# Layer 0's self-attention on one core: the places of the values' products and of the first-pass entries in TensorE's order

## The chip, the cores and the metric

The kernel runs on one core of a Trainium2 chip. The metric is the device time of one execution in microseconds (us), the median of several. TensorE is PE in the rows (PEld is its weight load), VectorE is DVE, ScalarE is ACT, GpSimd is POOL, and SP is the engine that issues most DMAs.

## What is computed

A two-layer decoder on x of 2 x 1024 x 256 with a context of 2 x 77 x 256. Each layer has self-attention, cross-attention and a mixture of experts, each behind a layer norm and added to x. Only layer 0's self-attention is touched; it has 16 heads of 16 elements, no mask, and a layer norm on each head's queries, keys and values:

```
q = _layernorm((x @ Wq + bq).reshape(b, s, NH, HD), q_scale, q_bias)
k = _layernorm((x @ Wk + bk).reshape(b, s, NH, HD), k_scale, k_bias)
v = _layernorm((x @ Wv + bv).reshape(b, s, NH, HD), v_scale, v_bias)
scores = jnp.einsum('bqhd,bkhd->bhqk', q, k) * HD ** (-0.5)
probs = jax.nn.softmax(scores, axis=-1)
out = jnp.einsum('bhqk,bkhd->bqhd', probs, v).reshape(b, s, NH * HD)
return out @ Wo + bo
```

## The kernel before

`attention(block, l, causal, ...)` (from line 793) builds the self-attention of both layers; layer 0 calls it with `causal=False`, layer 1 with `causal=True`. The work is cut into NU = 8 units, a unit being one sequence and G = 4 heads. Queries and keys are bf16 parts, stacked, so that one matmul over 96 rows gives the scores of a head at nearly fp32 accuracy.

A unit goes through two passes, and the first pass of one unit lies between the matmuls of the second pass of the unit before.

First pass: the maximum of each query's scores. It is made of entries in a list called `ring`, which PE and DVE take in the same order. A *fill* (`scores`, lines 927 to 939) is two matmuls of 512 columns (two heads, 128 queries, half the keys); DVE takes the maximum of each in one reduce (line 1119). A unit has 32 fills. After each 16 of them DVE makes the final maxima in three small steps (lines 1086 to 1098), PE turns them (*maxima*, `turn_maxima`, line 943), DVE copies them (line 1131) and SP stores them by four DMAs as two more rows of the query stack (line 891). The third kind of entry, *output* (`turn_output`, line 949), is four transposes of the finished sum of 512 queries, copied out of its bank by ACT (`copy_out`, line 1031); DVE normalizes it (lines 1106 and 1110). Entry n of the ring writes banks 2(n mod 2) and the next one, and may start when DVE is done with entry n-2 (line 958).

Second pass: 16 groups a unit (8 blocks of 128 keys for each half of 512 queries). In a group, for each of the 4 heads j, `second_pass` (line 974) makes one *score* matmul of 512 columns over 98 rows; the two additional rows subtract the maximum. ACT takes the exp of it (line 1040). Scores rotate over three banks, so a score waits for the exp three scores before it (line 972). When all four exps of a group are done, `weighted` (line 988) makes the *values' product* of that group: four heads side by side in the array, fp32, 8 instructions in the trace. It is issued one group late, behind the score with j = PV_AT.

PE's order is written out by hand (lines 1003 to 1017): ahead of each score it issues the ring up to `upto[u][gi * G + j]`. That list is built in lines 856 to 873. `goal` spreads the entries that are due by the end of a unit evenly over the unit's 64 places (in the first and last unit more of them early). Fills of the next unit begin in the unit before: in a unit 1 to 6, 32 fills, two maxima and two outputs are issued. By this rule a group has its fills either ahead of scores 0 and 2, or ahead of scores 1 and 3, and maxima take a place of their own, after which the two patterns change over. Outputs are put behind the entries of place j = 2 in groups 1 and 9. PV_AT is 1 in layer 0: the product comes behind the second score.

ACT takes the copy-out behind the exp of score j = OUT_AT = 2, in groups 0 and 8. PE waits for the rows of the first maxima at a unit's start, and for those of the second ahead of group 8.

SP's order in the stage: for each unit the rows of both maxima, then the loads of a later unit.

Of the kernel before, what the change touches and what calls it, by code (L numbers as in the profile page):

```python
# [32 lines left out]
G = 4  # L33
# [63 lines left out]
def build(nc, a, out):  # L97
    ctx = ExitStack()
    with ctx:
# [693 lines left out]
        def attention(block, l, causal, blocked=None, ahead=None):  # L793
# [23 lines left out]
            last_of = [max(i for i, g in enumerate(groups) if g[0] == half) for half in range(2)]  # L817
# [4 lines left out]
            def hilo(half):  # L822
                return mh[half].rearrange("p (j c t) -> p c j t", c=2, j=G)

            PV_AT = G - 1 if causal else 1
            OUT_AT = G - 1 if causal else 2
            FILL, MAX, OUT = range(3)
            feed = []
# [6 lines left out]
            due = []  # L835
# [5 lines left out]
            def goal(u, past):  # L841

                at0 = due[u - 1] if u else first_due
                if u in (0, NU - 1) and not causal:
                    soon = max(at0, feed.index((MAX, u, 1)) + 1)
                    if past <= early:
                        return at0 + round((soon - at0) * past / early)
                    return soon + round((due[u] - soon) * (past - early) / (1 - early))
                return at0 + round((due[u] - at0) * past)

            def width(gi):
                return BANK - groups[gi][2]
# [3 lines left out]
            ring = feed[:first_due]  # L856
            upto = [[] for _ in range(NU)]
            for u in range(NU):
                at0 = due[u - 1] if u else first_due
                at, past = at0, 0  # L860
                for gi in range(NGR):
                    for j in range(G):
                        past += width(gi) / G
                        upon = goal(u, past / WORK)
                        ring += feed[at:upon]
                        at = upon
                        if j == 2 and gi in (1, last_of[0] + 2):
                            half = 0 if gi > 1 else 1
                            if u or gi > 1:
                                ring.append((OUT, u if gi > 1 else u - 1, half))  # L870
                        upto[u].append(len(ring))
            ring += [(OUT, NU - 1, 1)]
            NR = len(ring)
            entry = {e: n for n, e in enumerate(ring)}
# [49 lines left out]
            def _(pe):  # L924
# [42 lines left out]
                def second_pass(u, gi, j):  # L967
                    r = u % NST
                    half, kt, lo = groups[gi]
                    n = (u * NGR + gi) * G + j  # L970
                    if n >= 3:
                        pe.wait_ge(*due_at("exp", n - 2))
                    bank = PS[:, 4 + n % 3, 0:BANK - lo]
                    pe.matmul(bank, kst[r][0:KM, j, kt * P:(kt + 1) * P], qst[r][0:KM, j, half * BANK + lo:(half + 1) * BANK],  # L974
                              start=True, stop=True).then_inc(sem(s + "_sc"), 1)

                def weighted(u, gi):
                    half, kt, lo = groups[gi]
                    if gi in diagonal:
                        pe.wait_ge(*due_at("past", u * len(diagonal) + diagonal.index(gi) + 1))  # L980
                    else:
                        pe.wait_ge(*due_at("exp", (u * NGR + gi + 1) * G))
                    if gi == 0:
                        pe.wait_ge(sem(f"{s}_v{u % NST}"), 16 * loads(l, u))
                    if kt == 0 and (u or half):
                        pe.wait_ge(*due_at("o", 2 * u + half))
                    for j in range(G):
                        mm = pe.matmul(PS[SLOT * j:SLOT * (j + 1), 7, lo:BANK], vst[u % NST][:, kt, j, :],  # L988
                                       prob[:, gi % 2 * G + j, lo:BANK], start=(kt == 0), stop=(gi == last_of[half]))
                    mm.then_inc(sem(s + "_pv"), 1)  # L990
# [12 lines left out]
                for u in range(NU):  # L1003
                    pe.wait_ge(*due_at("rows0", 16 * G * (u + 1)))
                    for gi in range(NGR):
# [3 lines left out]
                        for j in range(G):  # L1009
                            first_pass(upto[u][gi * G + j])  # L1010
                            second_pass(u, gi, j)
                            if j == PV_AT and gi:
                                weighted(u, gi - 1)
                            elif j == PV_AT and u:
                                weighted(u - 1, NGR - 1)
# [1899 lines left out]
        with nc.Block() as block:  # L2915
            prepare(block)
            ln(block, "ln03", "x_in", 16 * 4, banks=(6, 7))
            centre(block)
            turned, copied, blocked, valued = prepare_cross(block)
            qkv0(block, turned, copied, valued)  # L2920
            attention(block, 0, causal=False, blocked=blocked)
            ahead = cross_experts(block)
            attention(block, 1, causal=True, ahead=ahead)
# [29 lines left out]
```

## Time and profile before

| | us |
|---|---|
| median of 3 timed runs | 1839.29 (1837.18 to 1839.97) |
| the profiled execution | 1833.47 |
| its span, first to last instruction | 1831.6 |
| layer 0's self-attention, first score of unit 0 to last product | 147.50 to 549.45 |
| busy: PE, DVE, ACT, POOL | 1513.0, 1196.9, 977.4, 533.5 |

The profile is one execution. Times of rows are us from the start of the span. A row of the order of time gives the start, the duration, the engine and line, the operation and how many were merged (x2); behind it, in brackets, the idle time before it and what ended that. A merged row's duration runs from the start of its first to the end of its last instruction, and matmuls overlap: the end of one lies behind the start of the next. So for PE the distance from start to start is the measure.

### The profile page before, as it was taken

To read this page: it belongs to the slowest core of one execution; us is meant where nothing else is said; L and a number is where in the kernel's file an instruction comes from. 1 tells how busy PE (TensorE), PEld (TensorE's weight loads), DVE (VectorE), ACT (ScalarE), POOL (GpSimd) and SP (SyncE) were. 2 spreads that over 40 slices of the span, in tenths; PEclk is the share of its full clock that TensorE was granted. 3 is DMA by queue.
4 is the path that set the end of the run, shared out by engine and by line. 5 is a ranking of instruction groups with operands and counts; after the bars stand their busy time and mean duration, and the time that the engine had idled before them with its cause. 6 is when DMAs were issued, how large, how long until landed. Compare 5 with 4: busy or idle time off the path is not lost. (4 is left out here: it accounts for less than half of the span.)

```text
span 1831.6 us, 27871 instructions
## 1 busy us (share of the span) xinstructions
PE 1513.0 (83%) x8907; PEld 824.4 (45%) x8908; DVE 1196.9 (65%) x4538; ACT 977.4 (53%) x2014; POOL 533.5 (29%) x466
## 2 busy tenths in 40 slices
PE   5858999999985688888888779999987982389997
PEld 3512222222223466666665543333346761146665
DVE  6978877777715999999985167777615668311111
ACT  2835776677774566666666336666654551111121
POOL 1782000000001455556646452121211332331111
PEclk9968999999997899999999889999999995689999
DMA  7195223343000000000004535456120122621110
GB/s 218 58 232 73 32 34 100 43 93 47 1 27 1 1 1 1 1 1 2 1 2 96 106 127 71 65 102 89 43 92 1 18 41 41 221 95 40 49 42 6
DMA packets 116040, 106.02 MB, mean 58 GB/s; under 512 B 45811, under 2 KB 92987, under 8 KB 115902
## 3 DMA queue, kind: packets, MB, share of 16 engines
q1 hardware_dynamic: 110641, 93.83, 24.3%
q0 software_dynamic: 2640, 6.31, 0.9%
q10 hardware_dynamic: 2624, 4.19, 0.7%
q8 instruction: 69, 1.13, 0.3%
q14 instruction: 66, 0.54, 0.1%
HBM read 68.56 MB, written 36.41 MB: 57 GB/s over the span
## 5 line engine op out<-in xcount | busy, mean ns | idle before, releaser
L1119 DVE TENSOR_REDUCE arena<-banks 128x2 f32<-128x1024 f32 (+1 forms) x448 | 484.2, 1108 | 169.7 <-PE banks L935 114.9
L1040 ACT ACTIVATE arena<-banks 128x512 f32<-128x512 f32 (+3 forms) x896 | 444.5, 556 | 199.1 <-PE banks L974 192.8
L935 PE MATMUL banks<-arena 96*128 96x512 bf16 (+3 forms) x896 | 269.8, 377 | 42.4 <-DVE arena L1119 21.8
L974 PE MATMUL banks<-arena 98*128 98x512 bf16 (+3 forms) x896 | 273.1, 363 | 7.8 <-ACT arena L1040 7.8
L988 PE MATMUL banks<-arena 128*32 128x512 f32 (+3 forms) x1792 | 219.7, 562 | 13.1 <-ACT arena L1040 10.0
L2049 DVE MATCH_REPLACE8 arena<-arena 128x77 f32<-128x77 f32 x1024 | 213.9, 224 | 0.0
L935 PEld LDWEIGHTS banks<-arena 96*128 96x128 bf16 x896 | 77.5, 100 | 217.2 <-DVE arena L1119 128.6
L974 PEld LDWEIGHTS banks<-arena 98*128 98x128 bf16 x896 | 82.8, 98 | 180.1 <-ACT arena L1040 115.8
L2907 DVE COPY arena<-banks 128x1024 f32<-128x1024 f32 x23 | 28.2, 1225 | 197.2 <-PE banks L2841 197.2
L2041 DVE MAX8 arena<-arena 128x8 f32<-128x77 f32 x1024 | 149.6, 224 | 0.7
L1911 POOL TENSOR_SCALAR arena<-arena 128x256 f32<-128x256 f32 x32 | 17.8, 556 | 421.7 <-DVE arena L2029 421.7
L1908 POOL TENSOR_TENSOR arena<-arena 128x1232 f32<-128x1232 f32 x32 | 72.4, 2264 | 167.4 <-DVE arena L2049 165.8
L1636 PE MATMUL banks<-arena 128*128 128x256 f32 x512 | 116.7, 386 | 0.0
L1636 PEld LDWEIGHTS banks<-arena 128*128 128x128 f32 x512 | 97.1, 192 | 19.3 <-issue 5.9
L1071 POOL TENSOR_SCALAR_AFFINE_SELECT arena<-arena 128x512 f32<-128x512 f32 x64 | 40.7, 636 | 210.9 <-ACT arena L1040 210.7
L2856 PE MATMUL banks<-arena 128*128 x368 | 85.6, 385 | 1.4 <-DVE arena L2907 1.4
L2829 PE MATMUL banks<-arena 128*128 x184 | 84.5, 603 | 0.5 <-ACT arena L2881 0.5
L2049 DVE MATCH_VALUE_LOAD arena<-arena 128x8 f32 x1024 | 83.7, 82 | 1.7
L2856 PEld LDWEIGHTS banks<-arena 128*128 128x128 f32 x368 | 68.0, 190 | 19.3 <-issue 11.0
L2744 POOL DMA_INDIRECT decoded<-arena x23 | 22.6, 985 | 176.9 <-DVE arena L2899 175.4
L988 PEld LDWEIGHTS banks<-arena 128*32 128x32 f32 x1792 | 35.3, 108 | 84.1 <-ACT arena L1040 59.6
L2887 ACT ACTIVATE arena<-banks 128x1024 f32<-128x1024 f32 x23 | 23.6, 1024 | 86.1 <-PE banks L2832 86.1
(302 smaller groups left out, 2500.1 us busy)
## 6 DMA issues: line engine op xcount, KB each, us to landing
arena<-parts SPq DMA_DIRECT2D x192, 128.0 KB, 7.0
arena<-in_L_ffn_W SPq DMA_DIRECT2D x12, 1024.0 KB, 10.9
v<-arena SPq DMA_DIRECT2D x32, 256.0 KB, 3.4
arena<-v SPq DMA_DIRECT2D x16, 512.0 KB, 10.6
parts<-arena SPq DMA_DIRECT2D x12, 512.0 KB, 5.2
parts<-arena SPq DMA_DIRECT2D x16, 384.0 KB, 2.5
arena<-in_L_ffn_W ACTq DMA_DIRECT2D x4, 1024.0 KB, 9.5
arena<-sorted_rows SPq DMA_DIRECT2D x23, 129.0 KB, 2.2
```

What stands on the lines that cost most here:

```text
L935: mm = pe.matmul(bank[:, 0:w], qst[r][0:KS, j, i * P:(i + 1) * P], kst[r][0:KS, j, kb * BANK:kb * BANK + w], start=True, stop=not diag)
L974: pe.matmul(bank, kst[r][0:KM, j, kt * P:(kt + 1) * P], qst[r][0:KM, j, half * BANK + lo:(half + 1) * BANK], start=True, stop=True).then_i ...
L988: mm = pe.matmul(PS[SLOT * j:SLOT * (j + 1), 7, lo:BANK], vst[u % NST][:, kt, j, :], prob[:, gi % 2 * G + j, lo:BANK], start=(kt == 0), st ...
L1040: act.activation(prob[:, gi % 2 * G + j, lo:BANK], PS[:, 4 + n % 3, 0:BANK - lo], ACT.Exp, scale=SCALE).then_inc(sem(s + "_exp"), 1)
L1071: pool.affine_select(out=block_, in_=block_, compare_op=ALU.is_ge, fill=0.0, base=0, pattern=[[0, G], [1, P]], channel_multiplier=-1).then ...
L1119: dve.tensor_reduce(m2[u % 2][:, 2 * pair:2 * pair + 2, i, kb], PS[:, 2 * (n % 2):2 * (n % 2) + 2, 0:w], AX.X, ALU.max).then_inc(sem(s + " ...
L1636: mm = pe.matmul(PS[:, EB, 0:D], hmT[:, n, :], WeT[:, n // KD, n % KD, :], start=False, stop=(n == 2 * E - 1))
L1908: return pool.tensor_tensor(dst, src, m8[t % 2][:, 0, :, 0:1].to_broadcast([P, NH, C]), ALU.subtract)
L2041: dve.max(m8[r][:, k, hd, :], src[:, hd, :]).then_inc(sem(s + "_m" if k == 0 else f"{s}_m{k}"), 1)
L2049: dve.match_replace(out=left[r][:, hd, :], in_to_replace=m8[r][:, k, hd, :], in_values=src[:, hd, :], imm_value=LOWEST).then_inc(sem(f"{s} ...
L2829: pe.matmul(PS[:, 2 + half, :], xsT[r][:, k, :], W[:, bass.ds(e * EW + k * F + half * BANK, BANK)], start=(k == 0), stop=False)
L2856: pe.matmul(ps, lhs[:, k, :], weights[:, bass.ds(e * size + at + k * D, D)], start=(k == 0), stop=False)
```

## The change

Two things, in layer 0 alone (`not causal`); the order of layer 1 is built as before.

The values' product moves one score back: PV_AT is 2, so it stands behind the third score of a group.

The ring's entries no longer follow `goal`. A place `turned` takes entries up to and with the next fill; the others take none. Places with j = 3 are always turned; of the others j = 1, or j = 2 in a group with an output. In unit 0 groups 2, 5, 11 and 14 have j = 2 too (36 fills are due there). Outputs stand at j = 1 of groups 1 and 9, where there is no fill. Maxima come in the same place as the fill behind them: they are on top of the two fills of their group, where before they had a place of their own. A group is then: score 0; fill, score 1; score 2, product of the group before; fill, score 3. Group 4 and group 12 of units 1 to 6 have maxima and fill ahead of score 1. Groups 1 and 9: score 0; output, score 1; fill, score 2, product; fill, score 3. In unit 0 the first maxima entry in this stretch, the second of unit 0, moves from group 3 to group 5, into the place j = 2 of a group with three fills. In unit 7 all four fills are in groups 0 and 1, and the last maxima in group 2.

```diff
-            PV_AT = G - 1 if causal else 1
+            PV_AT = G - 1 if causal else 2
             OUT_AT = G - 1 if causal else 2
...
                 for gi in range(NGR):
                     for j in range(G):
                         past += width(gi) / G
+                        out = (OUT, u, 0) if gi == last_of[0] + 2 else (OUT, u - 1, 1) if gi == 1 and u else None
                         upon = goal(u, past / WORK)
+                        if not causal:
+
+
+                            upon = at
+                            turned = j == (2 if out else 1) or j == 3 or j == 2 and u == 0 and gi in (2, 5, 11, 14)
+                            while turned and upon < due[u]:
+                                upon += 1
+                                if feed[upon - 1][0] == FILL:
+                                    break
                         ring += feed[at:upon]
                         at = upon
-                        if j == 2 and gi in (1, last_of[0] + 2):
-                            half = 0 if gi > 1 else 1
-                            if u or gi > 1:
-                                ring.append((OUT, u if gi > 1 else u - 1, half))
+                        if out and j == (2 if causal else 1):
+                            ring.append(out)
                         upto[u].append(len(ring))
+                assert at == due[u]
```

## Rows read from the trace of the kernel before

**Rows 1.** Stretches (units 0, 3, 7, behind): PE, PEld, DVE, ACT, POOL busy, clock, DMA.
```profile
147.50:200.55 53.05, 50.34 (x263) 15.10 (x262) 43.58 (x47) 36.01 (x66) 1.20 (x1) 0.96 0.30 41
...
302.20:353.02 50.82, 47.77 (x268) 14.45 (x266) 40.01 (x45) 35.58 (x67) 0.00 (x0) 1.00 0.31 43
...
505.05:549.45 44.40, 37.69 (x211) 9.18 (x209) 8.13 (x13) 34.90 (x68) 0.00 (x0) 1.00 0.08 28
...
551.60:565.10 13.50, 9.06 (x26) 5.76 (x25) 0.85 (x3) 4.29 (x12) 1.16 (x2) 0.50 0.00 1
```

**Rows 2.** Order of time, PE, unit 3, output group: L974 score, L988 product, L935 fill.
```profile
305.03 0.60 PE L974 MATMUL banks<-arena 98*128 98x512 bf16 x2
306.21 1.06 PE L988 MATMUL banks<-arena 128*32 128x512 f32 x8 [0.58 <-ACT arena L1040]
307.21 0.61 PE L935 MATMUL banks<-arena 96*128 96x512 bf16 x2
...
308.09 0.60 PE L974 MATMUL banks<-arena 98*128 98x512 bf16 x2
309.14 0.60 PE L935 MATMUL banks<-arena 96*128 96x512 bf16 x2 [0.45 <-DVE arena L1119]
```

**Rows 3.** The same view, unit 3, around its maxima (L943).
```profile
315.07 0.23 PE L943 MATMUL banks<-arena 128*32 128x128 bf16 x1
315.23 0.39 PE L974 MATMUL banks<-arena 98*128 98x512 bf16 x1
316.03 0.61 PE L935 MATMUL banks<-arena 96*128 96x512 bf16 x2 [0.40 <-DVE arena L1119]
```

**Rows 4.** The same view, unit 3, groups without a stall.
```profile
319.31 0.38 PE L974 MATMUL banks<-arena 98*128 98x512 bf16 x1
319.62 1.07 PE L988 MATMUL banks<-arena 128*32 128x512 f32 x8
320.62 0.39 PE L974 MATMUL banks<-arena 98*128 98x512 bf16 x1
...
322.46 0.64 PE L988 MATMUL banks<-arena 128*32 128x512 f32 x4
```

**Rows 5.** Order of time, DVE, unit 3: reduces of fills.
```profile
307.85 1.23 DVE L1119 TENSOR_REDUCE arena<-banks 128x2 f32<-128x1024 f32 x1 [1.13 <-PE banks L935]
...
314.75 1.23 DVE L1119 TENSOR_REDUCE arena<-banks 128x2 f32<-128x1024 f32 x1 [0.48 <-PE banks L935]
```

**Rows 6.** Order of time, ACT, unit 3: copy-out (L1031) and exps (L1040).
```profile
305.08 0.58 ACT L1031 COPY arena<-banks 128x512 f32<-128x512 f32 x1
305.54 1.60 ACT L1040 ACTIVATE arena<-banks 128x512 f32<-128x512 f32 x3
308.51 1.09 ACT L1040 ACTIVATE arena<-banks 128x512 f32<-128x512 f32 x2 [1.37 <-PE banks L974]
```

**Rows 7.** Order of time, PE's weight loads: that of the second score of 305.03.
```profile
305.23 0.10 PEld L974 LDWEIGHTS banks<-arena 98*128 98x128 bf16 x1 [0.32 <-ACT arena L1040]
```

**Rows 8.** Order of time, PE and DVE, unit 7.
```profile
513.97 1.23 DVE L1119 TENSOR_REDUCE arena<-banks 128x2 f32<-128x1024 f32 x1 [1.12 <-PE banks L935]
...
515.98 0.22 PE L943 MATMUL banks<-arena 128*32 128x128 bf16 x1
...
517.69 1.06 PE L988 MATMUL banks<-arena 128*32 128x512 f32 x8
...
519.77 0.39 PE L974 MATMUL banks<-arena 98*128 98x512 bf16 x1 [0.26 <-ACT arena L1040]
520.26 1.06 PE L988 MATMUL banks<-arena 128*32 128x512 f32 x8
```

**Rows 9.** Order of time, SP and PE, start of the stage.
```profile
142.07 2.76 SPq L891 DMA_DIRECT2D arena<-arena  x4
...
146.72 1.01 PE L935 MATMUL banks<-arena 96*128 96x512 bf16 x2 [0.28 <-DMA arena<-arena]
...
152.94 0.64 PE L988 MATMUL banks<-arena 128*32 128x512 f32 x4
```

## The prediction

> **What bounds the kernel now.** I read the busy time of each engine by stretch first. The change touches layer 0's self-attention alone, so the question is which engine sets the length of one of its eight units. Unit 3 takes 50.82 us, with PE busy 47.77, DVE 40.01 and ACT 35.58 at the full clock of 2.4 GHz (granted 1.00) [rows 1]. PE is the bound, but 3.05 us are still idle in it, and its ends are modelled. So I went to the PE's own order of time and measured from start to start. A 512-column score or fill matmul is followed by the next one after 0.22 us (a fill, which is two of them, takes 0.44); a values' product that nothing holds up comes 0.31 after the score before it and lets the next matmul start 1.00 later; a group without a stall repeats after 2.84 us (319.62 to 322.46) [rows 2, 4]. Output transposes take 0.44: 307.21 to 308.09 is a fill (0.44) and four transposes [rows 2]. Maxima take 0.09 + 0.16 = 0.25 [rows 3]. A unit without stalls is then 16 x 2.84 + 2 x 0.44 + 2 x 0.25 = 46.8 us, so the unit of 50.82 holds 4.0 us of stalls. They stand at four places, two of each kind:
> - Output group (two a unit): scores at 305.03 and 305.25, so the product is due at 305.56 and comes at 306.21: 0.65. It waits for ACT, which put the copy-out (305.08) ahead of the group's last exp (305.54). Then the scores at 308.09 and 308.31 make the fill due at 308.53; it comes at 309.14: 0.60 to 0.61, waiting for DVE [rows 2, 6].
> - Maxima group (two a unit): maxima at 315.07, a score at 315.23, fill due at 315.45, comes at 316.03: 0.58 [rows 3]. What is left of the 4.0, some 0.17 each time, I put to the product of the pair order (two scores next to each other ahead of it, so that it needs a late exp).
>
> Both fill stalls are the same rule in the code: entry n of the ring may start when DVE is done with entry n-2. Reading a fill takes 1.23 us, starts 0.42 after the second matmul of the fill has started (307.85 against 307.43), and PE goes on 0.06 after its end: 314.75 + 1.23 + 0.06 is 316.03 [rows 2, 3, 5]. So a fill is ready 0.42 + 1.23 + 0.06 = 1.70 us after the second matmul of the fill two entries before it.
>
> **The change, part by part.** It adds and removes no instruction; it moves them on PE and, with the ring, on DVE. The new group on PE is: score 0, fill, score 1, score 2, product of the group before, fill, score 3.
>
> Plain group (12 of a unit's 16). From score 0: fill 0.22, score 1 0.65, score 2 0.87, product 0.87 + 0.31 = 1.18, fill 2.18, score 3 2.62, next score 0 2.84. That is the old stall-free length: nothing won. Three waits have to be hidden. Product: the last exp of the group before starts 0.42 after its score (308.51 against 308.09) and lets PE go 0.67 after it starts (305.54 to 306.21) [rows 2, 6]: score 3 stood at -0.22, so the product may go at 0.87, long before 1.18. Fills: ready 1.70 after the one before them at -0.44, that is 1.26, against 2.18; the other has more. Score 2 needs the bank that the group before's score 3 used (three banks): its exp ends at -0.22 + 0.42 + 0.60 = 0.80, and PE can go 0.05 later, 0.85; score 2 is due at 0.87. That margin is 0.02 and nothing covers it. The old order has the same spacing once in some groups: there the weight load of the score due at 305.25 waited for ACT until 305.23, and the matmul was not late [rows 2, 7]. I take zero.
> The Trainium skill (TensorE: Matmul & The Clock Gate, Step-by-step: what each phase is for) says that PE pulls weight loads ahead of matmuls in flight. If that were needed here, a load that waits until 0.85 and takes 0.10 would make every score 2 late by about 0.08; the row of 305.23 disagrees, the matmul going 0.02 behind the start of its load.
>
> Output group. The copy-out now waits on ACT for a product one place later. The product (start 1.18, 1.06 long) lets ACT go at about 2.28; ACT, with exps 0.5 apart, is free at 2.18, copies from 2.28 to 2.86 and can start the next instruction 0.46 after the copy's start (305.08 to 305.54), at 2.74, before the next exp is due at 2.62 + 0.42 = 3.04 [rows 2, 6]. Queued behind the waiting copy is only that exp, so the 0.65 goes. The transposes are due at 3.06, with the copy ready at 2.92: no wait. The fill now comes behind fill, score 3, score 0, four transposes, score 1: from the second matmul of the earlier fill 0.22 + 0.22 + 0.22 + 0.44 + 0.22 = 1.31, ready at 1.70: stall 0.39, in place of 0.60. Together 0.39 for 1.26 [rows 2, 6].
>
> Maxima group. Maxima and a fill stand in one slot: from the earlier fill's second matmul score 3 0.22, score 0 0.44, maxima 0.75, fill 0.91, ready 1.70: stall 0.79. Old 0.58 + 0.17. A loss of 0.04 each [rows 3, 5].
>
> Per unit: 2 x 0.39 + 2 x 0.79 = 2.35 of stalls for 4.0 (3.98 from the finer starts): 1.63 us less, so 49.2 us. Six units (1 to 6): 9.8 us. Bounds: the output's fill between 0 and the old 0.60, the maxima's between the old 0.58 and 0.79 plus one more 0.22: the six units give between 9.8 - 5.2 = 4.6 and 9.8 + 4.7 + 2.5 = 17; I take the worked-out values, since each is a sum of spacings seen next to each other in rows 2 to 5.
>
> Unit 0 runs its first 4.6 us at half clock (granted 0.96 over the unit), 0.43 a matmul [rows 1, 9]. The first entry stood at 146.72, held by the maxima's row DMAs; now score 0 stands there, and 13 matmuls (0.43 each, one of them 0.38) later the first product comes at 152.3 instead of 152.94, with two fills fewer behind it: 0.64 - 0.87 = -0.2. From 152.94 to the unit's end at 200.55 are 47.6 us; the work in it (15 products, 58 scores, 32 fills, an output, two maxima, at the spacings above) is 43.9, the stalls 3.7. The new order has 0.39 in the output group, 0.39 in each of three groups with three fills (one stands a group's end, 1.31, behind the fill two entries before it), about 1.3 where maxima and a fill stand two places behind another fill, and 0.1 at the other maxima: 3.0. Net gain 0.5. The second maxima of unit 0 move two groups later; their rows must land in the 7 us before group 8, and four such DMAs took 2.76 to issue and had landed 4.6 after the first issue [rows 9]. Unit 2's loads, queued behind them on SP, start some 6 us later; they are wanted by unit 2's first fill, in group 2 of unit 1, over 30 us on: no cost.
>
> Unit 7 has fills in its first groups only. Old: the product of group 3 comes 12.64 into the unit (517.69 against 505.05), the last product at 44.40, so 31.76 later [rows 1, 8]; the cycle is 2.57 (517.69 to 520.26). New: group 0 is 2.84 and the output group 2.84 + 0.44 + 0.39; the last fill's second matmul stands at 6.08, and the last maxima right behind it. From the start of that reduce to the maxima 2.01 pass in DVE's steps (513.97 to 515.98), so they come at 6.08 + 0.42 + 2.01 = 8.51, a stall of 1.68. Score 1, score 2, product, score 3 follow at 8.67, 8.89, 9.20, 10.20; its exp starts 0.42 later, lets score 2 go after 0.65 and the product 0.31 after that: 11.6. That last chain is the new cycle, 1.00 + 0.42 + 0.65 + 0.31 = 2.38, so the product of group 3 comes at 13.96, 1.3 late. From there eleven cycles, 2.08 to the last product (it needs no score 2) and about 0.3 for an output that waits for its copy make 28.6 in place of 31.76. Net gain 1.8.
>
> Sum: 9.8 (six units) + 0.5 + 1.8 = 12.1 us. The profiled execution had 1833.47 us around its span of 1831.6; 1821.4 by this. The three timed runs have a median of 1839.29, 0.3% more, and I carry the difference over: 1827.2 us. What follows, layer 0's cross-attention, starts from the last output transposes and should move as a block.
>
> **The rivals.** (1) The gain is partly given back behind the stage. PE falls to half clock (granted 0.50) for 13.5 us there with 9.06 busy [rows 1]; one more such stretch, because PE's idle times meet it otherwise, costs 4.5 us. For it: the clock changes at times that are not tied to the work; against: it may as well save one. 1830 to 1834.
> (2) Score 2 pays for its late bank: 0.08 in each of 112 groups, 9.0 us, gain 3: 1836.3. Against it stands rows 7.
> (3) Slower: the same score pays the load and then the 0.09 that a product pays on top of 0.22, 0.17 a group, 19 us: 1846. It decides from 12.1 / 112 = 0.11 us a group on.
> (4) The order doesn't do what it says: DVE, not the slot, sets the output and maxima stalls, so they only move: 1838 to 1840. Against: DVE needs 40.0 of 50.8 us.
>
> **How the numbers follow.** About 0.2% (3.7 us) is what can be told from no change. Forecast, 1824 to 1830: 0.75. (1) 0.10. (2) 0.06. (3) 0.05. (4) 0.04. Faster 0.85, same 0.10, slower 0.05. The range is 1824 to 1833.5: the forecast's case and most of (1).
>
> **What would show it.** Unit starts 49.2 us apart; a copy-out that begins right at the product's end, with no product waiting for ACT behind it; fills by 0.39 late in output groups and 0.79 in maxima groups; unit 7's cycle 2.38, maxima by 1.7 late there. A plain group over 2.84 is rivals (2) or (3), to be seen at score 2. The stage's last product should end 12 us earlier; if it does and the total doesn't, it is (1). The forecast is wrong if a wait that I hold hidden appears, above all score 2's.

## The result, and the profile after

The changed kernel takes 1824.35 us (median of 4, 1823.76 to 1825.56), the kernel before 1838.45 in the same comparison (median of 4, 1837.18 to 1839.97). The ratio is 0.9924 with a 95% interval of 0.9907 to 0.9941: 14.1 us or 0.76% faster. Forecast were 1827.2 us and 12.1 us less, with a range of 1824 to 1833.5; the measured time lies 0.35 us above the lower end of that range.

The two profiled executions tell another number, 1833.47 and 1824.05, only 9.4 us. So the profile has to be read in pieces. The first rows are times from the start of the span, the others are lengths; a unit is measured from its first score.

| us | before | after | difference | forecast |
|---|---|---|---|---|
| first product of unit 0 starts | 152.94 | 151.57 | -1.4 | -0.6 |
| unit 1 starts | 200.55 | 198.67 | -1.9 | -0.5 |
| last product of the stage starts | 549.45 | 536.59 | -12.9 | -12.1 |
| units 1 to 5, each | 50.82 | 49.17 | -1.65 | -1.63 |
| unit 6 | 50.39 | 49.17 | -1.2 | -1.63 |
| unit 7, first score to last product | 44.40 | 42.92 | -1.5 | -1.8 |
| last output transpose to layer 1's first score | 544.4 | 542.0 | -2.4 | 0 |
| from there to the first tile of the last stage | 511.7 | 512.0 | +0.3 | 0 |
| last stage (layer 1's experts) | 223.8 | 229.5 | +5.7 | 0 |

The stretches that answer to rows 1 (columns as there: length, busy time and instructions of PE, PEld, DVE, ACT, POOL, then the granted clock, DMA share and GB/s), of the kernel after; units 0, 3 and 7, and behind the stage:

```profile
146.70:198.67 51.97, 49.60 (x262) 14.92 (x263) 43.59 (x47) 35.10 (x65) 1.73 (x2) 0.96 0.31 41
297.00:346.17 49.17, 47.28 (x267) 14.31 (x266) 40.01 (x45) 34.68 (x66) 0.00 (x0) 1.00 0.32 44
493.67:536.59 42.92, 37.03 (x210) 8.94 (x208) 8.04 (x13) 35.07 (x67) 0.00 (x0) 1.00 0.08 29
536.60:546.60 10.00, 4.98 (x26) 2.82 (x27) 0.85 (x3) 4.07 (x10) 0.89 (x2) 1.00 0.00 1
546.80:550.00 3.20, 2.74 (x11) 2.05 (x10) 0.00 (x0) 0.80 (x3) 0.06 (x1) 0.50 0.00 0
```

PE in order of time, unit 3 of the kernel after: L983 score, L944 fill, L997 product, L958 output, L952 maxima. First a plain group and the output group, then the maxima group.

```profile
297.65 0.59 PE L983 MATMUL banks<-arena 98*128 98x512 bf16 x2
298.18 1.06 PE L997 MATMUL banks<-arena 128*32 128x512 f32 x8
299.18 0.61 PE L944 MATMUL banks<-arena 96*128 96x512 bf16 x2
299.62 0.60 PE L983 MATMUL banks<-arena 98*128 98x512 bf16 x2
300.05 0.61 PE L958 MATMUL banks<-arena 128*128 128x128 f32 x4
300.50 0.38 PE L983 MATMUL banks<-arena 98*128 98x512 bf16 x1
301.10 0.61 PE L944 MATMUL banks<-arena 96*128 96x512 bf16 x2 [0.22 <-DVE arena L1128]
301.55 0.38 PE L983 MATMUL banks<-arena 98*128 98x512 bf16 x1
301.86 1.06 PE L997 MATMUL banks<-arena 128*32 128x512 f32 x8
...
304.69 1.07 PE L997 MATMUL banks<-arena 128*32 128x512 f32 x8
...
307.53 1.06 PE L997 MATMUL banks<-arena 128*32 128x512 f32 x8
308.53 0.61 PE L944 MATMUL banks<-arena 96*128 96x512 bf16 x2
308.97 0.59 PE L983 MATMUL banks<-arena 98*128 98x512 bf16 x2
309.50 0.23 PE L952 MATMUL banks<-arena 128*32 128x128 bf16 x1
310.45 0.61 PE L944 MATMUL banks<-arena 96*128 96x512 bf16 x2 [0.73 <-DVE arena L1128]
```

Where rows 2 had a product 0.65 late and a fill 0.60 late, the products now come 0.31 behind the score before them, and one fill is late: due at 300.50 + 0.22 = 300.72, it comes at 301.10, 0.38. In the maxima group (rows 3: 0.58) the fill is due 0.16 behind the maxima, at 309.66, and comes at 310.45, 0.79 or 0.80 by the rounding. Both are 1.70 us after the second matmul of the fill two entries before: 299.18 + 0.23 + 1.70 = 301.11, and 308.53 + 0.23 + 1.70 = 310.46. Plain groups repeat after 2.84 (304.69 to 307.53), as in rows 4. Nothing else is late in the unit.

ACT in order of time, the same place (L1040 copy-out, L1049 exp), and the weight load of score 2:

```profile
297.20 2.07 ACT L1049 ACTIVATE arena<-banks 128x512 f32<-128x512 f32 x4 [0.77 <-PE banks L983]
299.31 0.58 ACT L1040 COPY arena<-banks 128x512 f32<-128x512 f32 x1
300.04 1.58 ACT L1049 ACTIVATE arena<-banks 128x512 f32<-128x512 f32 x3
```

```profile
297.85 0.10 PEld L983 LDWEIGHTS banks<-arena 98*128 98x128 bf16 x1 [0.32 <-ACT arena L1049]
```

The copy-out starts 1.13 after its product and is over before the next exp is due (rows 6 had an exp held up by it). Score 2 started at 297.65 + 0.22 = 297.87, 0.02 behind its weight load, which had waited for the exp: the margin of 0.02 holds, as it did in rows 7 of the kernel before.

Unit 7 of the kernel after, the last maxima and the cycle:

```profile
502.18 0.22 PE L952 MATMUL banks<-arena 128*32 128x128 bf16 x1 [1.61 <-DVE arena L1107]
...
505.26 1.06 PE L997 MATMUL banks<-arena 128*32 128x512 f32 x8
...
507.34 0.39 PE L983 MATMUL banks<-arena 98*128 98x512 bf16 x1 [0.26 <-ACT arena L1049]
507.66 1.06 PE L997 MATMUL banks<-arena 128*32 128x512 f32 x8
```

The maxima come 8.51 us into the unit (502.18 - 493.67), 1.68 late; the cycle is 2.40 (rows 8: 2.57).

### The profile page after: what moved, and what is told of

It is laid out like the page before. It is cut to its first block and busy times, and to the rows that moved or that the text cites. A ratio compares the mean times of both kernels' runs of the same rounds, so it can differ in the third digit from the quotient of the medians.

```text
span 1822.3 us, 27871 instructions
## 1 busy us (share of the span) xinstructions
PE 1506.7 (83%) x8907; PEld 823.0 (45%) x8908; DVE 1197.1 (66%) x4538; ACT 971.0 (53%) x2014; POOL 533.7 (29%) x466
## 3 DMA queue, kind: packets, MB, share of 16 engines
q8 instruction: 69, 1.13, 0.3%
## 5 line engine op out<-in xcount | busy, mean ns | idle before, releaser
L1049 ACT ACTIVATE arena<-banks 128x512 f32<-128x512 f32 (+3 forms) x896 | 435.4, 557 | 192.4 <-PE banks L983 188.0
L944 PE MATMUL banks<-arena 96*128 96x512 bf16 (+3 forms) x896 | 269.5, 377 | 44.8 <-DVE arena L1128 23.5
L983 PE MATMUL banks<-arena 98*128 98x512 bf16 (+3 forms) x896 | 263.9, 362 | 8.2 <-ACT arena L1049 7.8
L997 PE MATMUL banks<-arena 128*32 128x512 f32 (+3 forms) x1792 | 219.5, 562 | 1.2 <-ACT arena L1049 0.7
L944 PEld LDWEIGHTS banks<-arena 96*128 96x128 bf16 x896 | 72.6, 100 | 253.6 <-issue 110.3
L983 PEld LDWEIGHTS banks<-arena 98*128 98x128 bf16 x896 | 83.3, 98 | 155.9 <-ACT arena L1049 87.3
L1917 POOL TENSOR_TENSOR arena<-arena 128x1232 f32<-128x1232 f32 x32 | 72.4, 2262 | 167.5 <-DVE arena L2058 165.9
L2372 POOL TENSOR_TENSOR arena<-arena 128x1232 f32<-128x1232 f32 x16 | 36.2, 2266 | 113.6 <-DVE arena L2432 113.6
## 6 DMA issues: line engine op xcount, KB each, us to landing
arena<-v SPq DMA_DIRECT2D x16, 512.0 KB, 10.7
parts<-arena SPq DMA_DIRECT2D x12, 512.0 KB, 5.2
```

The costliest lines, as they stand in the source:

```text
L944: mm = pe.matmul(bank[:, 0:w], qst[r][0:KS, j, i * P:(i + 1) * P], kst[r][0:KS, j, kb * BANK:kb * BANK + w], start=True, stop=not diag)
L1049: act.activation(prob[:, gi % 2 * G + j, lo:BANK], PS[:, 4 + n % 3, 0:BANK - lo], ACT.Exp, scale=SCALE).then_inc(sem(s + "_exp"), 1)
L1917: return pool.tensor_tensor(dst, src, m8[t % 2][:, 0, :, 0:1].to_broadcast([P, NH, C]), ALU.subtract)
```

## The experiments

The theory: a stall of PE in this stage is what is left of 1.70 us after the second matmul of the fill two entries before it, or of the wait for ACT; the order of PE's work decides which entries are late, and the waits add up without hiding each other, since PE is the bound. Rivals: the fixed pattern of the entries is what wins, or the product's place; and, for what is not in the stage, that the change causes it, or that the execution does.

### The same two kernels again

Edit: none, the kernel before and the kernel after.

> The kernel before, unchanged, to see what of the difference outside layer 0's self-attention belongs to the change and what to the single execution. In the two profiles the stage ends 12.9 us earlier after the change, the next stage gives another 2.4, and the start of the last stage (layer 1's experts) takes 5.8 back. Theory A (these two are chance of the execution, not of the change): the stage is again 50.82 us a unit; behind it the length of the half-clock stretch at the start of the cross-attention (13.7 us before, 3.4 after) and the 5.8 us at the start of layer 1's experts come out differently in some repeat of the same kernel; the timed runs of before lie 4 to 6 us above its profile because most of them had the 5.8. Theory B (they follow from the change): this profile again has 13.7 us at half clock there and no loss at the experts, span within 1 us of 1831.6.

> The changed kernel, unchanged. Theory A (chance of the execution): units again 49.17 us apart, but the half-clock stretch behind the stage or the 5.8 us at the start of layer 1's experts may differ from the first profile. Theory B (follows from the change): 3.4 us at half clock behind the stage and 5.8 us lost at the experts again, span within 1 us of 1822.3.

Measured: 1839.61 and 1823.38 us. The units are 50.82 and 49.16 apart. From the last output transpose to layer 1's first score the kernel before took 544.4 again, the one after 541.7 where its first execution had 542.0. But the last stage took 229.4 in this execution of the kernel before. The stretches of it in both executions of before, then in the first of after:

```profile
1607.80:1831.60 223.80, 211.60 (x851) 130.57 (x851) 37.34 (x46) 40.76 (x69) 36.33 (x38) 0.97 0.15 45
```

```profile
1608.40:1837.80 229.40, 213.15 (x851) 131.70 (x851) 37.33 (x46) 40.60 (x69) 36.31 (x38) 0.97 0.14 44
```

```profile
1592.80:1822.30 229.50, 213.15 (x851) 131.84 (x851) 37.33 (x46) 40.61 (x69) 36.24 (x38) 0.97 0.14 44
```

So the 5.7 us belong to the execution: 223.8 was the exception, and it was the profile shown ahead of the prediction. Eleven of the thirteen profiles of this study have 229.3 to 229.6 there, one 223.8 and one 233.7. Theory A holds for this part. The other came out as theory B has it: the 2.4 us behind the stage were there both times. But two executions of each kernel are few, and the repeats further down show that this stretch can differ between executions of one kernel.

The stage itself isn't free of such chance either. In the second execution of the changed kernel it began 1.5 us earlier (first score at 145.17 for 146.70) and still ended at 536.60, because unit 7 took 44.08 us for 42.92: the granted clock was 0.50 for 3.40 us from 501.6 on. PE had just waited 1.68 us for the last maxima, until 501.02; in the first execution the same wait had no such stretch behind it.

```profile
501.60:505.00 3.40, 3.40 (x13) 0.59 (x12) 0.00 (x0) 1.84 (x4) 0.00 (x0) 0.50 0.01 2
```

### The product alone

```diff
-            PV_AT = G - 1 if causal else 1
+            PV_AT = G - 1 if causal else 2
```

> Only the values' product behind the third score, the ring in its old places. Theory A (stalls follow from the spacing of the entries, n-2 rule and 1.70 us): the copy-out no longer holds up the product (old 0.65 twice a unit, gone), the fill behind an output no longer waits (the product lies between), but the output comes 0.65 to 1.1 behind the fill two entries before it and waits about 0.6; at the maxima the product or a whole group's end lies between, no wait. So 1.2 us of stalls a unit, units 48.0 us apart, less than the 49.17 of the full change: 5 to 8 us faster than the changed kernel, 1816 to 1820 us. Rival (the fixed pattern of entries is what wins): units near 50.5, total within 3 us of the kernel before.

Measured: 1820.42 us (median of 4), ratio to the kernel before 0.9901, 95% interval 0.9884 to 0.9917. So the smaller edit wins more than the full change, 17.3 us, though the time is 0.4 us above what was expected. The stage ends at 532.49, 4.1 us before that of the full change. (The profiled execution is the slowest of the four, 1824.70: layer 1 up to its last stage took 515.6 us in it, where the twelve other profiles have 511.1 to 512.1.) The units are 48.76 apart, not 48.0. PE in order of time (L974 score, L935 fill, L988 product, L949 output):

```profile
295.14 0.60 PE L935 MATMUL banks<-arena 96*128 96x512 bf16 x2
295.58 0.38 PE L974 MATMUL banks<-arena 98*128 98x512 bf16 x1
295.80 0.59 PE L935 MATMUL banks<-arena 96*128 96x512 bf16 x2
296.23 0.60 PE L974 MATMUL banks<-arena 98*128 98x512 bf16 x2
297.06 0.61 PE L935 MATMUL banks<-arena 96*128 96x512 bf16 x2 [0.24 <-DVE arena L1119]
...
299.91 0.60 PE L935 MATMUL banks<-arena 96*128 96x512 bf16 x2
300.96 0.66 PE L949 MATMUL banks<-arena 128*128 128x128 f32 x4 [0.45 <-DVE arena L1119]
```

The output waits 0.61 (due at 300.35, comes at 300.96), as worked out. The 0.39 at 297.06 I had missed: where the ring goes over from fills ahead of scores 1 and 3 to fills ahead of scores 0 and 2, which happens twice a unit, two fills stand one score apart (295.14 and 295.80) with no product behind them, and the next fill is due at 296.67, before 295.36 + 1.70 = 297.06. 2 x 0.61 + 2 x 0.39 = 2.0 on 46.8 are the 48.8.

### The pattern alone

The whole change but for the product, which stays behind the second score:

```diff
-            PV_AT = G - 1 if causal else 2
+            PV_AT = G - 1 if causal else 1
```

> Only the ring's fixed places, the product behind the second score as before. Theory A: in an output group the output waits about 0.45 us for its copy-out and nothing else waits; in a maxima group the fill on top waits 0.79: 2.5 us of stalls a unit in place of 3.98, units 49.3 us apart. Unit 7 keeps its cycle of 2.57 and gets the maxima's stall of about 1.7, some 1 us slower than before. In all 7 to 10 us faster than before, 1828 to 1832 us. Rival (the gain is the product's place): units 50.5 or more, total as before.

Measured: 1837.53 us (median of 10), ratio 0.9999, 95% interval 0.9988 to 1.0009: nothing that the runs can tell. The expectation of 7 to 10 us was wrong. In the profile the stage ends at 548.22, 1.2 us before that of the kernel before: unit 0 and its earlier start win 0.9 us, units 1 to 6 win 2.3, and unit 7 loses 2.0. The stretches of unit 4 and unit 7, and PE around an output and maxima (L983 score, L944 fill, L997 product, L958 output, L952 maxima):

```profile
350.71:401.07 50.36, 47.66 (x267) 14.37 (x266) 40.00 (x45) 36.22 (x67) 0.00 (x0) 1.00 0.45 84
501.81:548.22 46.41, 37.88 (x210) 9.02 (x209) 8.04 (x13) 35.23 (x68) 0.00 (x0) 1.00 0.08 26
```

```profile
354.31 0.63 PE L958 MATMUL banks<-arena 128*128 128x128 f32 x4 [0.39 <-ACT arena L1040]
...
356.08 0.61 PE L944 MATMUL banks<-arena 96*128 96x512 bf16 x2
...
358.01 0.61 PE L944 MATMUL banks<-arena 96*128 96x512 bf16 x2 [0.24 <-DVE arena L1128]
...
364.75 0.61 PE L944 MATMUL banks<-arena 96*128 96x512 bf16 x2 [0.73 <-DVE arena L1128]
```

The output waits 0.54 for its copy-out (expected 0.45) and the maxima's fill 0.80, as foreseen; but the fill at 358.01 waits 0.39 too, 1.70 after 356.31, because with the product ahead of both fills of the output group nothing long stands behind them. Units are 50.36 apart in place of 49.3, and unit 7 is 2.0 us longer than before, where some 1 us was expected. The rule gives the missed wait; I had not applied it to that fill.

### Maxima, outputs and the last maxima moved on

On top of the full change: maxima one fill later, so that they stand ahead of score 3;

```diff
-                feed.insert(feed.index((FILL, u, HALF_FILLS - 1)) + 5, (MAX, u, 0))
-                feed.insert(feed.index((FILL, u, NF - 1)) + (5 if u < NU - 1 else 1), (MAX, u, 1))
+                late = 5 if causal else 6
+                feed.insert(feed.index((FILL, u, HALF_FILLS - 1)) + late, (MAX, u, 0))
+                feed.insert(feed.index((FILL, u, NF - 1)) + (late if u < NU - 1 else 1), (MAX, u, 1))
```

outputs ahead of the fill of score 3;

```diff
-                            turned = j == (2 if out else 1) or j == 3 or j == 2 and u == 0 and gi in (2, 5, 11, 14)
+                            turned = j == 1 or j == 3 or j == 2 and u == 0 and gi in (2, 5, 11, 14)
...
+                        if out and j == 3 and not causal:
+                            ring.append(out)
                         ring += feed[at:upon]
                         at = upon
-                        if out and j == (2 if causal else 1):
+                        if out and j == 2 and causal:
                             ring.append(out)
```

and unit 7's last maxima in group 3:

```diff
+                            turned = turned and not (u == NU - 1 and gi == 2)
                             while turned and upon < due[u]:
```

> The changed kernel with each maxima entry put one fill later in layer 0, so that it stands in the place ahead of score 3, behind the product, instead of ahead of score 1. Theory A (a stall is what is left of 1.70 us after the second matmul of the fill two entries before): the product now lies between, the fill on top waits 0.06 in place of 0.80, nothing else comes late; units 47.7 us apart in place of 49.17, unit 0 about 1 us shorter, 9 to 10 us off the changed kernel at the end of the stage. Rival (the stall moves on: a shorter ring wait shows up as a wait of the scores or the product for ACT): units above 48.6.

> The changed kernel with the output entries put ahead of the fill of score 3 in groups 1 and 9, the fills back at scores 1 and 3. Theory A: the fill that waited 0.38 in each output group waits no more; the first fill of the next group waits for DVE's two steps of the output, about 0.1. Units 48.6 us apart, 3 to 4 us off the changed kernel at the end of the stage. Rival (DVE's reciprocal and product of the output, then two reduces, come late in a row): units 49.2 or more.

> The changed kernel with unit 7's last maxima one group later (group 3). Theory A: they come at 8.5 us into the unit by DVE's three steps in any case; group 2 runs meanwhile and the stall of 1.68 goes: unit 7 from its first score to its last product 41.3 us in place of 42.9, all units before it as in the changed kernel. Rival (the rows of these maxima come late for group 8): unit 7 as before or longer, with PE waiting for a DMA ahead of group 8.

> The three moves together: maxima and outputs ahead of the fill of score 3, unit 7's last maxima in group 3. Theory A: stalls of 0.06 and 0.1, units 47.2 us apart, unit 7 about 41 us; the stage ends near 521 us in the profile, 15 us before the changed kernel, and the total is 1805 to 1813 us, depending on where the half-clock stretches fall behind the stage. Rival (PE is then so full that ACT's last exp or the copy-out comes late): units above 48.

| | median us | ratio to before, 95% interval | units apart | unit 7 | last product |
|---|---|---|---|---|---|
| maxima moved | 1815.71 | 0.9879 (0.9860 to 0.9899) | 47.49 | 42.92 | 528.60 |
| outputs moved | 1821.14 | 0.9916 (0.9901 to 0.9931) | 48.68 | 42.97 | 533.34 |
| last maxima moved | 1832.14, again 1821.51 | one run each, no interval | 49.16 | 41.42 | 539.34, again 534.65 |
| all three | 1812.03 | 0.9860 (0.9842 to 0.9878) | 47.00 | 41.28 | 522.92 |

All four distances of units are within 0.21 us of what was expected, and each move's gain appears in full beside the others': 49.17 - 1.68 - 0.49 = 47.00. Of the waits in a unit only one is left, a fill 0.10 late in each output group, as expected of the outputs' move; none of PE for ACT took the place of those removed. The last maxima's move takes 1.5 us off unit 7 in both of its executions; with one run each the total doesn't show it.

Where the stage ends was missed twice. With the maxima moved it ends 8.0 us before that of the changed kernel, not 9 to 10: PE was at half clock until 155.6 in that execution, in the changed kernel until 150.7, and unit 0 took 54.15 us for 51.97. With all three it ends 13.7 us earlier, not 15. PE with the maxima moved (L998 product, L953 maxima, L945 fill), and the stretch of unit 3 with all three:

```profile
309.08 1.06 PE L998 MATMUL banks<-arena 128*32 128x512 f32 x8
309.96 0.22 PE L953 MATMUL banks<-arena 128*32 128x128 bf16 x1
310.30 0.61 PE L945 MATMUL banks<-arena 96*128 96x512 bf16 x2
```

```profile
293.64:340.64 47.00, 46.76 (x267) 14.64 (x266) 39.81 (x45) 34.25 (x66) 0.00 (x0) 1.00 0.32 46
```

Maxima behind a product start 0.88 after it, where a fill starts 1.00 after it, and the fill follows 0.34 behind them: they cost 0.22, a little less than the 0.25 of rows 3. All three together are 12 us below the changed kernel and 1.4% below the kernel before: this version beats both, and the product alone too.

### What moved outside the stage

> The kernel of last_max, unchanged. In its profile unit 7 was 1.5 us shorter as expected, but the stage started 2 us late, PE stayed 3.4 us longer at half clock in unit 0, and the last stage took 233.7 us from its first tile to the end where nine other profiles have 229.5 or 223.7: 1832.1 in all. Theory A (all three are chance of that execution): unit 7 again 41.4 us, the half-clock stretch at the start 44 to 48 us, the last stage 229.5 or 223.7, total 1819 to 1825. Theory B (the edit does it): again 51 us at half clock and 233.7 in the last stage, 1831 or more.

> The kernel of pv_alone, unchanged. From the stage's last output transpose to the first score of layer 1 it took 543.2 us (two half-clock stretches of 3.4 near the stage's end), where the kernel before took 544.4 in both profiles and the changed kernel 542.0 and 541.7. Theory A (this time is fixed by the kernel, through where the changes of the clock fall against the end of the stage, whose time from the rise of the clock on is fixed): again 543.0 to 543.4. Theory B (chance of the execution): anything from 541.7 to 544.4.

> The kernel of all_three, unchanged. From the stage's last output transpose to the first score of layer 1 it took 543.7 us, with 10.2 us at half clock behind the stage. Theory A (fixed by the kernel): again 543.5 to 543.9 and 10.2 us. Theory B (chance): as likely near 542.

Measured: 1821.51, 1821.05 and 1813.02 us. Unit 7 of the first is 41.42 again, the last stage 229.6: the 10.6 us between its two executions were 47.8 against 51.2 us at half clock at the start with a stage that began over 3 us earlier, 1.2 behind the stage, and 4.1 in the last stage. Theory A holds there.

From the last output transpose to layer 1's first score, the kernel with all three moves took 543.9 after 543.7 with 10.2 us at half clock again, as theory A has it. The product alone took 544.0 after 543.2, outside the 543.0 to 543.4 of theory A, which falls there; the last maxima's move took 541.9 after 543.1. So the kernel doesn't fix this time. What goes with it in all thirteen profiles is how long PE is at half clock in the 20 us behind the stage:

| us at half clock | executions | last output transpose to layer 1's first score, us |
|---|---|---|
| 3.4 | the changed kernel twice; pattern alone, maxima moved, outputs moved; last maxima moved, the second | 541.7 to 542.4 |
| 6.8 | product alone, the first; last maxima moved, the first | 543.1 to 543.2 |
| 10.2 | product alone, the second; all three twice | 543.7 to 544.0 |
| 13.7 | the kernel before twice (rows 1, its last line) | 544.4 |

Two kernels changed rows between their two executions. What sets the length is open, and whether the change had a part in its own 2.4 us is not shown.

The last stage's loss, ACT in order of time in the kernel after; the second row is the copy that waits for two transposes of PE, which by the trace started at 1602.59:

```profile
1600.57 1.02 ACT L2896 ACTIVATE arena<-banks 128x1024 f32<-128x1024 f32 x1 [6.22 <-PE banks L2841]
1608.11 0.37 ACT L2890 COPY arena<-banks 128x256 f32<-128x256 f32 x1 [6.51 <-remote]
1613.85 1.02 ACT L2896 ACTIVATE arena<-banks 128x1024 f32<-128x1024 f32 x1 [5.37 <-remote]
```

ACT waited for 6.5 and 5.4 us, and the trace names no releaser in the core for it. POOL was issuing indirect DMAs then, in the good execution too. Its cause stays open; no run here varied that stage.

## Why the prediction was right, and where not

**The bound and the stalls.** Right to 0.03 us a unit: 49.17 for 49.2, with a fill 0.38 late (forecast 0.39) and one 0.79 or 0.80 late (0.79), no product waiting, plain groups 2.84. Units 1 to 5 gave 1.65 us each. Unit 6 gave only 1.2: I had taken 50.82 us for all six, but in the kernel before unit 6 has one fill fewer from its first score on and took 50.39. The six gave 9.5 us for 9.8. The stretch of unit 6 in the kernel before:

```profile
454.66:505.05 50.39, 47.34 (x265) 14.25 (x264) 39.58 (x45) 35.20 (x66) 0.00 (x0) 1.00 0.00 1
```

**Score 2's margin.** Right; rivals (2) and (3) fall. By the Trainium skill (TensorE: Matmul & The Clock Gate, Step-by-step: what each phase is for) the load is pulled ahead of matmuls in flight. The trace agrees, and the lead can be as small as 0.02 us without the matmul being late: the load began at 297.85, 0.20 behind the start of the matmul in flight, and its own matmul at 297.87.

**Unit 7.** The maxima came at 8.51 us into the unit as worked out, the product of group 3 at 13.99 (13.96). From there the cycle was 2.40 for 2.38, and the last product came at 42.92 for 42.56: net gain 1.5, not 1.8. The chain of 0.42 from score to exp was taken from a score behind a score; behind a product it is 0.43, and eleven cycles of 0.02 more are 0.2 of the difference. The rest is the output, which costs 0.45 on top of its cycle (products at 517.26 and 520.11) where I had put 0.3.

**Unit 0.** Mis-sized: forecast 0.5, measured 1.9, from two causes of 0.7 each. The first product came at 151.57, not at 152.3, because PE's clock rose to 2.4 GHz at 150.7, while the first fill of group 1 ran (150.49, then 151.05), where before it rose at 152.2; I had assumed the same moment. The stretch at half clock that ends there took 47.8 us in both executions of before and 44.4 in both of after, but 51.2 and 47.8 in the two of the kernel with the last maxima moved, so these 0.7 us may be luck. And from the first product to unit 1 the unit took 47.10 us, where the forecast's terms give 47.8: I had charged two fills more behind the first product (0.87), but up to the first score of unit 1 it is one fill more and one score fewer (33 and 57 in the trace, 32 and 58 before), 0.22.

**The sum.** 12.1 for the stage's 12.9 is closer than its terms: unit 0 gave 1.4 more than forecast, the six units 0.3 less and unit 7 0.3 less.

**Carried over to the median.** This step was not sound. I took the 0.3% between profile and median for a constant. Most of it is as large as the last stage's 5.7 us, absent from the one profiled execution of before and present in the twelve other profiles; the timed runs have no profile, so that it was in them too is argued, not shown. The total was saved because I applied the difference in microseconds to the median, not to the profile: the profile moved by 9.4.

**Rival (1).** It was named with its price, 4.5 us for a half-clock stretch of 13.5; it came with the other sign, 2.4 us saved. With it 12.9 + 2.4 make the 15.3 that the pieces give before the last stage; the medians say 14.1. The rival's reason, that the clock changes at times not tied to the work, fits the two kernels whose stretches differed between executions. By the pieces, 12.9 less the 0.7 of the clock in unit 0 is 12.2 for the forecast's 12.1; what the change seems to win beyond that lies in the clock, here and in unit 0, and not in the mechanism. It was partly luck, then, that brought the time so near the lower end of the range; the kernel before also came 0.8 lower in the second comparison (1838.45 for 1839.29).

**What the sum did not show.** Two parts of opposite worth. The product's place won 17.3 us alone; the pattern on top of it cost about 4 (the stage ends at 532.5 and 532.0 without it, at 536.6 twice with it) and alone did nothing that the runs can tell. I priced the maxima's step as a small loss against the old order, which was right, but I did not price it against the order with only the product moved, where that stall isn't there at all.

## What to carry to other kernels

Where two engines share a ring of two slots, measure once how long an entry takes from its last instruction to the release of its slot (here 1.70 us), then read the stalls off the order itself, and put the longest piece of other work (here the product, 1.00 us) between an entry and the one two places behind it. Price each edit against the order without it, not against the old one: a part that removes one stall and sets another can hide behind a part that wins. And profile the kernel before more than once: one stretch of a single execution differed by 5.7 us, 0.4 of the gain.

## What the runs showed of the hardware

- A matmul can start 0.02 us after its own weight load has started, though the load is recorded with 0.10 (297.85 and 297.87).
- At full clock the time from the start of the last matmul into a bank or bank pair to the start of the engine that waits for it is 0.42 to 0.43 us, for VectorE and ScalarE alike and in all thirteen profiles; back from that engine's end to PE it is 0.05 to 0.06.
- A product of four heads side by side costs 1.00 us to the next score, but only 0.88 to bf16 transposes of 128 columns (309.08 to 309.96).
- The stretch at half clock (granted 0.50) behind the stage was 3.4, 6.8, 10.2 or 13.7 us long, and the time from there to layer 1's first score went with it, from 541.7 to 544.4 us. Two executions of one kernel had different lengths in two of five kernels.
